# Maxima and reciprocals of a gated attention block, carried to all lanes by DMA over memory instead of by TensorE

## What is computed

```python
q = (query @ Wq + bq).reshape(B, L, NKV, G, HDIM)
k_, v_ = jnp.split(kv @ Wkv + bkv, 2, axis=-1)
scores = jnp.einsum('blkgd,bmkd->bkglm', q, k) * scale
attn = jax.nn.softmax(scores, axis=-1)
o = jnp.einsum('bkglm,bmkd->blkgd', attn, v).reshape(B, L, NHEAD * HDIM)
x = x + jnp.tanh(g_xattn[0]) * (o @ Wo + bo)
x = x + jnp.tanh(g_ffn[0]) * ffn(layernorm(x))
```

## Time and profile before

| | us |
|---|---|
| median of 3 runs | 2336.55 |
| range of the runs | 2336.43 to 2344.85 |
| the profiled execution, whole | 2337.85 |
| its span in the profile | 2335.9 |
| PE busy | 2289.8 |
| DVE busy | 1822.1 |
| ACT busy | 1685.2 |
| POOL busy | 1631.9 |

### The profile page before, as it was taken

One profiled execution on the slowest core, in us unless ns is written; L12 is line 12 of the kernel. 1 busy time (PEld: TensorE's weight loads), 2 busy tenths in 40 slices (PEclk: granted clock), 3 DMA queues, 4 the chain that ended last, 5 costly groups with the idle time before them and its releaser, 6 DMA issues.

```text
span 2335.9 us, 37750 instructions
## 1 busy us (share of the span) xinstructions
PE 2289.8 (98%) x12569; PEld 1956.9 (84%) x12569; DVE 1822.1 (78%) x3162; ACT 1685.2 (72%) x3208; POOL 1631.9 (70%) x1372
## 2 busy tenths in 40 slices
PE   7999999999999999999999999999999999999988
PEld 6888888888888888888888888888888888888864
DVE  5887888879778787877878778787878768778775
ACT  4776777767777776777767777776777767777763
POOL 5897987967667786866757867774865757656672
PEclk9999999999999999999999999999999999999999
DMA  7444334354133233335133243223423122122211
GB/s 256 147 147 142 117 129 144 133 201 144 59 124 114 93 122 100 98 108 185 59 104 105 77 133 115 102 92 115 143 82 109 66 79 82 46 100 73 82 37 54
DMA packets 122591, 258.11 MB, mean 111 GB/s; under 512 B 13344, under 2 KB 46624, under 8 KB 122144
## 3 DMA queue, kind: packets, MB, share of 16 engines
q1 hardware_dynamic: 122400, 255.71, 32.4%
HBM read 188.81 MB, written 66.86 MB: 109 GB/s over the span
## 4 chain that ended last, share of the span: by engine, by line
PE 87%; DVE 5%; POOL 4%; ACT 2%; issue 2%; DMA 0%; ACTq 0%; SPq 0%; POOLq 0%; DVEq 0%
PE psW L381 13%; PE psW L382 12%; PE psW L383 12%; PE psW L577 7%; PE psS L383 7%; PE psS L381 7%; PE psS L382 7%; PE psW L579 7%; PE psW L578 7%; PE psW L436 2%; PE psW L444 2%; POOL xs L766 2%; POOL pl L770 1%; DVE mrun L1194 1%; DVE psum_ L1221 1%
## 5 line engine op out<-in xcount | busy, mean ns | idle before, releaser
L766 POOL TENSOR_TENSOR xs<-xs,mb 128x512 f32<-128x512 f32 (+1 forms) x832 | 1069.2, 1314 | 518.1 <-ACT mb L837 518.1
L1194 DVE TENSOR_TENSOR mrun<-psS,mrun 128x512 f32<-128x512 f32 (+1 forms) x704 | 483.9, 687 | 380.3 <-ACT xs L837 377.7
L837 ACT ACTIVATE xs<-psS 128x512 f32<-128x512 f32 (+1 forms) x832 | 496.7, 597 | 212.2 <-PE psS L383 202.6
L930 ACT ACTIVATE ph<-xs 128x512 fp32r<-128x512 f32 (+1 forms) x832 | 520.6, 626 | 0.9 <-PE psW L579 0.9
L991 DVE TENSOR_TENSOR pl<-psP,ph 128x512 fp32r<-128x512 f32 (+1 forms) x672 | 459.5, 684 | 54.8 <-ACT ph L930 49.0
L1221 DVE TENSOR_TENSOR psum_<-psP,psum_ 128x512 f32<-128x512 f32 (+1 forms) x672 | 457.3, 681 | 0.0
L927 ACT ACTIVATE psP<-xs 128x512 f32<-128x512 f32 (+1 forms) x672 | 402.4, 599 | 3.0 <-POOL xs L766 1.5
L381 PE MATMUL psS<-ql,kh 128*128 128x512 f32 (+1 forms) x832 | 344.1, 414 | 1.1 <-DVE ql L1014 1.1
L577 PE MATMUL psW<-ph,vh 128*128 128x512 f32 (+1 forms) x832 | 336.6, 405 | 5.8 <-POOL pl L770 4.0
L383 PE MATMUL psS<-qh,kl 128*128 128x512 f32 (+1 forms) x832 | 328.1, 394 | 0.0
L382 PE MATMUL psS<-qh,kh 128*128 128x512 f32 (+1 forms) x832 | 328.1, 394 | 0.0
(11 more groups left out here) (185 smaller groups left out, 4562.5 us busy)
## 6 DMA issues: line engine op xcount, KB each, us to landing
wqh<-scr_wq SPq DMA_DIRECT2D x96, 256.0 KB, 2.6
wql<-scr_wq SPq DMA_DIRECT2D x96, 256.0 KB, 2.9
woh<-scr_wo SPq DMA_DIRECT2D x48, 512.0 KB, 3.3
wol<-scr_wo SPq DMA_DIRECT2D x48, 512.0 KB, 4.4
scr_wq<-wqh SPq DMA_DIRECT2D x32, 256.0 KB, 2.0
scr_wq<-wql SPq DMA_DIRECT2D x32, 256.0 KB, 2.5
scr_wo<-woh SPq DMA_DIRECT2D x16, 512.0 KB, 2.6
scr_wo<-wol SPq DMA_DIRECT2D x16, 512.0 KB, 4.0
```

The lines of the kernel that those rows point to most:

```text
L766: eng.tensor_tensor(tile, tile, mb[0:rows_of(t), U % 2, :], ALU.subtract).then_inc(s_sub)
L837: return eng.activation(hi, src, ACT.Copy)
L930: eng.activation(ph[0:rows, T % RP, :], xs[0:rows, T % RX, :], ACT.Exp).then_inc(s_h)
L1194: eng.tensor_tensor(run, psS[0:rows, s % 2, :], a, ALU.max).then_inc(s_m)
```

## The change

For units 2 to 61 the job `b` and for units 2 to 60 the job `r` go. In their place SP writes `nm` (or `rinv`) to a small scratch in memory, `scr_m` (or `scr_r`), waits until it has landed, and reads it back with one DMA that gives every lane the whole row of 512 values. For this the row must come out in the order of the queries: `turn` now takes every fourth column of its source, so that lane `p` holds the four neighbouring queries `4 p` to `4 p + 3`. POOL waits for the landing of the DMA (`s_md`) instead of ACT's copy, DVE for `s_rd`. DVE makes these two reductions at the head of a slot, ahead of its running maximum. The unit's output is normalised in slot 9 instead of slot 8, and `o0` is always in slot 11. The strings of stretches 4 to 62 are new.

```diff
+    AT_MEM = [
+        "m q0 k3 - q1 s v0 v1 v2 v3 - o0 o1",
+        "m,v4 v5 q0 v6 k0 s,v7 q1 k1 v8 v9 v10 o0 o1",
+        "m,v11 k2 v12 q0 k3 s - - q1 - - o0,x0 o1,x1",
+        "m q0 - k0 q1 s k1 - - k2 - o0 o1",
+    ]
...
-            def turn(key, src, done, by, v):
+            def turn(key, src, done, by, v, every_fourth=False):
                 o = take(key)
                 for k in range(4):
-                    m = eng.transpose(o[:, k * 128:(k + 1) * 128], src[:, k * 128:(k + 1) * 128], ident[:, :])
+                    cols = src.rearrange("l (p k) -> l k p", k=4)[:, k, :] if every_fourth else src[:, k * 128:(k + 1) * 128]
+                    m = eng.transpose(o[:, k * 128:(k + 1) * 128], cols, ident[:, :])
...
+            def max_to_lanes(n):
+
+                i = n - MEM_LO
+                sp.wait_ge(s_nm, n + 1)
+                if i >= 2:
+                    sp.wait_ge(s_md, 16 * (i - 1))
+                eng.dma_start(scr_m[n % 2], nm[:, n % 2, :]).then_inc(s_mw, 16)
+                sp.wait_ge(s_mw, 16 * (i + 1))
+                if n >= 2:
+                    sp.wait_ge(s_sub, NT * (n - 1))
+                eng.dma_start(mb[:, n % 2, :], scr_m[n % 2].rearrange("p k -> (p k)").partition_broadcast(128)).then_inc(s_md, 16)
...
+                if t == 1 and max_by_mem(U - 1):
+                    max_to_lanes(U - 1)
+                if t == 6 and sum_by_mem(U - 2):
+                    sum_to_lanes(U - 2)
...
-                pool.wait_ge(s_mb, U + 1)
+                if max_by_mem(U):
+                    pool.wait_ge(s_md, 16 * (U - MEM_LO + 1))
+                else:
+                    pool.wait_ge(s_mb, by_pe(U, max_by_mem))
...
+                for j in jobs.get(s - 1, []):
+                    if goes_first(*j):
+                        after_job(*j)
...
-                if t == 8 and 0 <= U - 2 < UN:
-                    V = U - 2
+                V = U - 2
+                if 0 <= V < UN and t == on_slot(V):
                     dve.wait_ge(s_pv, NT * (V + 1))
-                    dve.wait_ge(s_rb, V + 1)
+                    if sum_by_mem(V):
+                        dve.wait_ge(s_rd, 16 * (V - MEM_LO + 1))
```

More of the change, by code:

```diff
@@ L19, in gated_block @@
 def gated_block(nc: bass.Bass, x, ctxT, gx, gf, wq, bq, wk, wv, bkv, wo, bo, bw, rw, la, lb,
-                scr_x, scr_b, scr_w, scr_c, out):
+                scr_x, scr_b, scr_w, scr_c, scr_m, scr_r, out):
     F32 = mybir.dt.float32
@@ L52, in lead, with max_by_mem, sum_by_mem, by_pe @@
         return 1 if U < NU else 3
+    MEM_LO, MEM_MAX, MEM_SUM = 2, UN - 2, UN - 3
+    def max_by_mem(U):
+        return MEM_LO <= U < MEM_MAX
+    def sum_by_mem(U):
+        return MEM_LO <= U < MEM_SUM
+    def by_pe(U, by_mem):
+        return sum(not by_mem(u) for u in range(U + 1))
+    def on_slot(V):
+        return 9 if sum_by_mem(V) else 8
     jobs = {s: [] for s in range(SLOTS)}
@@ L61, in gated_block @@
     ]
+    AT_MEM = [
[4 rows of a table added]
+    ]
     for U in range(UN + 2):
         names_of = {0: "k1 - k2 v0 q0 k3 q1 v1 - v2 - v3 -", UN: "- - - - - s - r - - o0 - o1",
-                    UN + 1: "- - - - - s - r - - o0 o1"}.get(U, AT[U % 4])
+                    UN + 1: "- - - - - s - r - - o0 o1"}.get(U, (AT_MEM if U >= 2 and sum_by_mem(U - 2) else AT)[U % 4])
         for t, names in enumerate(names_of.split()):
@@ L71, in gated_block @@
                 if not 0 <= n < top or (kind == "x" and U % NU < 14):
+                    continue
+                if kind == "b" and max_by_mem(n) or kind == "r" and sum_by_mem(n):
                     continue
@@ L221, in gated_block @@
         s_out = sem("s_out")
+        s_mw = sem("s_mw")
+        s_md = sem("s_md")
+        s_rw = sem("s_rw")
+        s_rd = sem("s_rd")
         s_s = sem("s_s")
@@ L505, in job @@
                     pe.wait_ge(s_m, 12 * (n + 1))
-                    turn(("m", n, 0), mrun[:, n % 2, :], s_mt, s_nm, n + 1)
+                    turn(("m", n, 0), mrun[:, n % 2, :], s_mt, s_nm, n + 1, max_by_mem(n))
                 elif kind == "s":
@@ L513, in job @@
                         pe.wait_ge(s_ap, 2 * (n - NU + 1))
-                    turn(("s", n, 0), psum_[:, n % 2, :], s_su, s_r, n + 1)
+                    turn(("s", n, 0), psum_[:, n % 2, :], s_su, s_r, n + 1, sum_by_mem(n))
                 elif kind == "b":
                     pe.wait_ge(s_nm, n + 1)
-                    spread(("b", n, 0), nm[:, n % 2, :], s_bt, s_mb, n + 1)
+                    spread(("b", n, 0), nm[:, n % 2, :], s_bt, s_mb, by_pe(n, max_by_mem))
                 elif kind == "r":
                     pe.wait_ge(s_r, n + 1)
-                    spread(("r", n, 0), rinv[:, n % 2, :], s_rt, s_rb, n + 1)
+                    spread(("r", n, 0), rinv[:, n % 2, :], s_rt, s_rb, by_pe(n, sum_by_mem))
                 elif kind == "x":
@@ L579, in _ @@
                     eng.matmul(o, vl[0:rows, t, hs], hi, start=False, stop=t == NT - 1).then_inc(s_pv)
-                if s % NT == 10 and s // NT >= 2:
+                if s // NT >= 2 and s % NT == on_slot(s // NT - 2) + 2:
                     emptied(("pv", s // NT - 2, 0), s_ol, s // NT - 1)
@@ L648, in load_ctx, with sum_to_lanes @@
                 eng.dma_start(f32(cl[:, :, lo:lo + w]), scr_c[b - 1, 1, :, :, lo:lo + w]).then_inc(s_lc[c], 16)
+            def max_to_lanes(n):
[8 more added lines that the diff above has]
+                eng.dma_start(mb[:, n % 2, :], scr_m[n % 2].rearrange("p k -> (p k)").partition_broadcast(128)).then_inc(s_md, 16)
+            def sum_to_lanes(n):
+                i = n - MEM_LO
+                sp.wait_ge(s_r, n + 1)
+                if i >= 2:
+                    sp.wait_ge(s_rd, 16 * (i - 1))
+                eng.dma_start(scr_r[n % 2], rinv[:, n % 2, :]).then_inc(s_rw, 16)
+                sp.wait_ge(s_rw, 16 * (i + 1))
+                if n:
+                    sp.wait_ge(s_on, n)
+                eng.dma_start(rbc[:, :], scr_r[n % 2].rearrange("p k -> (p k)").partition_broadcast(128)).then_inc(s_rd, 16)
             eng.dma_start(x_raw, x[:, 0:2, :]).then_inc(s_in["x"], 16)
@@ L956, in _ @@
                 V = s // NT - 2
-                if s % NT == 8 and 0 <= V < UN:
+                if 0 <= V < UN and s % NT == on_slot(V):
                     act.wait_ge(s_on, V + 1)
@@ L1178, in _, with goes_first @@
             dve.wait_ge(s_tg, 1)
+            def goes_first(kind, n, part):
+                return kind == "m" and max_by_mem(n) or kind == "s" and sum_by_mem(n)
             for s in range(SLOTS):
@@ L1205, in _ @@
                 for j in jobs.get(s - 1, []):
-                    if j[0] not in "ms" or not TN - NT < s <= TN:
+                    if (j[0] not in "ms" or not TN - NT < s <= TN) and not goes_first(*j):
                         after_job(*j)
@@ L1228, in _ @@
                     for j in jobs[s]:
-                        if j[0] in "ms":
+                        if j[0] in "ms" and not goes_first(*j):
                             after_job(*j)
```

18 lines of the change are left out of this document (12 added, 6 removed).

## The result

The changed kernel takes 2455.14 us (median of 4 runs, 2448.71 to 2462.12), the kernel before 2339.14 us on the same chip. The ratio is 1.0493, with a 95% interval of 1.0456 to 1.0530. It is slower by 116 us, where I had forecast 40 us less.

What follows compares the result with a forecast made beforehand. PE's own work was taken as the bound: 2337.85 - 52.4 - 6.8 + 7 + 4 + 3 + 6 = 2298.7 us profiled, 1.3 above the median, so 2297; own range 2282 to 2314 (chance 0.52), wider range 2282 to 2343.

Steps and rivals of the forecast that it cites:

- What goes, 52.4 us: On PE: 60 jobs `b` and 59 jobs `r` removed, 119 x 0.44 = 52.4 us saved.
- the new order in type 1, 6.8 us: Slot `o0,v8` of type 1: one job per slot ends a bank wait, 0.45 us in 15 stretches, 6.8 saved.
- The rival that DVE takes the bound: In runs of slots without jobs DVE holds PE: 24 us back, 2321; chance 0.17, shared with a small stride price.
- The strided load at nothing: PE's weight loads of the turned tile, 16-byte step: 0 us extra taken; upper bound 67 us kept as a rival.
- The write at 1.7 us: SP's 2 KB write to memory: lands after 1.7 us, taken between 1.4 and 2.0.
- The read at 2.6 us: Read back to all lanes, filling 256 KB: 2.6 us, as the loads of `wqh` take.
- 7 + 4 + 3 us: Late maxima: 7 us in type 3, 4 in type 0 where context is stored, 3 for batch 0's weight cuts.
- Room at `L0` and `L2`: Delay that fits before PE's products: 0.93 us at `L0`, 1.24 at `L2`; stall of 0.5 us per type 3 stretch.
- The rival of a longer round trip: Each further us of delay costs 28 us in types 3 and 0; at 6.3 us, 2359; within the 0.11 above 2348.
- `o0` "now stands a slot later and has it in time": Type 2: `o0`'s wait for `ol`, about 0.4 us, goes; taken with 0.44 us given back at `L2`'s product as 0.
- The reciprocal elsewhere: Away from batch ends: it takes 4.4 us from slot 6, needed in slot 9, more than 5 us on.
- Ends of batches at 2 us each: Three batch ends: `ch` and `cl` stand in the reciprocal's way; DVE and PE wait 2 us each, 6 us.

## Why the prediction was wrong, by its own steps

- **What goes, 52.4 us, and the new order in type 1, 6.8 us: right in size.** Type 1 shows both: 1.0 to 1.2 us a stretch for the 1.33 of the sum, and 3.8 in stretch 57, which makes 20.3 for 20.0 by luck. The rival that DVE takes the bound did not come: slots without jobs take 1.38 to 1.48 us in U = 55.
- **The strided load at nothing: nearly right.** Loads grew from 140 to 200 ns, the slot by 0.03 us, 2 to 4 us over 119 turns. The Trainium skill, Advanced Engine Details and Errata, SBUF Cachelines, has a penalty for reads that touch a different 16-byte line each time. The trace agrees (the 60 ns), and shows that nearly all of it is hidden here.
- **The write at 1.7 us: right only where nothing stands ahead.** Undisturbed it took 1.4 us, the lower end that I had drawn from the rows. In the stretches of batches 1 and 2 where contexts are stored it took 2.8 to 4.4 us, and in batch ends 7.4 to 10. I had priced the stores at 0.6 us, and in type 0 alone, though type 3 has them too (U = 39, +5.9 us).
- **The read at 2.6 us: the step that failed first.** I took the duration of a load of as many bytes, though the trace had no read of one row by all lanes but `in_bo`, 6.2 us, which I put aside. It took 4.5. Together with the write the maxima start POOL at 10.6 to 11 us in quiet stretches, not 8.9. With the stall behind it, 7 + 4 + 3 us in the sum, types 0 and 3 came out at +93 us, where the forecast has 28 x 0.88 less and 14 more, so -10.6.
- **Room at `L0` and `L2`: right in type 3, wrong in type 0.** The rule found, length = start of POOL + 23.0, gives 31.9 us for the forecast start, 0.5 above the 31.4 without a stall: my very number, though I had it at `L2` and PE now waits at job `s` and at `L0`. With the measured 11.04 it gives 34.04; less 0.44 for `r`, plus 0.63 for `o0`, that is 34.23, and 34.27 was measured. But type 0 has no more room than type 3 (8.35 us against 8.4), and I had charged it only where contexts are stored. The rival of a longer round trip named 28 us for each microsecond, which is the slope found, and put 2359 at 6.3 us. At the 6.6 us of U = 55 it gives 62 of the 104 us by which types 0 and 3 missed; the rest I put down to the stores, the room in type 0 and the lower clock, without having parted them. For type 2 I had "several us of room" in one place and 1.3 in another; with the maxima alone by DMA it lost nothing.
- **`o0` "now stands a slot later and has it in time": wrong.** I counted slots, not microseconds. The slots ahead of it had become short, and it waits 0.4, 0.6 and 1.65 us in types 0, 3 and 2. I also never asked what moving `k3` to slot 2 does to DVE's additions and so to POOL's merge.
- **The reciprocal elsewhere: in time, as forecast.** In U = 54 it lands 0.5 us after the start of slot 9, and DVE begins to normalise 2.1 us after it, as in the stretches where it came earlier.
- **Ends of batches at 2 us each: right place, four times too small.** Three cost 6.6 to 9.9 us. The last batch's, with the loads for the experts, cost 7.9, and I had not counted it. The small write lands late behind the big loads, PE stands at the product behind DVE rather than at `o0`, and its idle time is followed by the lower clock.
- **What no step had:** long stalls of PE are paid twice. The mean granted clock fell from 0.996 to 0.978 over the span, which is at most 44 of the 116 us.
- **The range.** Its lower end, 2282, does not follow from its own terms: without the 7 and the 6 us the sum gives 2284, without the 4 and the 3 as well 2277. It changes nothing here.

## What to carry to other kernels

A transfer in place of a computation must be costed from issue to use, in the very form that it will have: its row pattern, and what stands ahead of it on the same queue at each place. Compare that with the room of each place by itself. Here the same edit is worth -1.2 us in one kind of stretch and +1 to +6 in another, and keeping it only where the results still come in time turned +116 us into -30. When jobs move among slots of unequal length, count microseconds from the producer to the consumer, not slots.
